# Who issues the roll: the two partition-shift transfers of q, k and v move from SyncE's queue to ScalarE's

## The reference

```python
def _to_quaternion(x):                       # x: (B, S, 16 heads, 8)
    p1 = jnp.diff(x, axis=1, prepend=x[:, :1])   # difference along the sequence
    p2 = jnp.roll(x, 1, axis=2)                  # heads shifted by one
    p3 = jnp.cos(x)
    return jnp.stack([x, p1, p2, p3], axis=-1)

qkv = (x @ aw + ab).reshape(B, S, H, 3 * HD)
q, k, v = jnp.split(qkv, 3, axis=-1)
qk = _hamilton(_to_quaternion(q), _to_quaternion(k))
qkv_p = _hamilton(qk, _to_quaternion(v))
... # spectral filter over positions and heads, projection, residual, norm, feed-forward
x = L0_attn_x
xn = _layernorm(x)
x = x + _L0_attn_ref(xn, ...) + _L0_ffn_ref(xn, ...)
xn = _layernorm(x)
x = x + _L1_attn_ref(xn, ...) + _L1_ffn_ref(xn, ...)
```

## Time and profile before

| | |
|---|---|
| median of three runs | 1510.28 us (1504.66 to 1510.45) |
| the profiled execution's own time | 1511.32 us |
| its span | 1509.5 us |
| granted TensorE clock, mean | 0.977 |
| PE busy | 1401.4 us (93%) |
| DVE busy | 1253.8 us (83%) |
| ACT busy | 1044.0 us (69%) |
| POOL busy | 356.2 us (24%) |

### The profile page before, as it was taken

The page is one execution under the profiler, slowest core; times in us unless marked ns, Lnnn a source line. Parts: engine busy times, 40 slices in busy tenths (PEclk is TensorE's granted clock), DMA queues, the critical chain, the costliest instruction groups (busy, mean ns, idle before and its releaser), DMA issues.

```text
span 1509.5 us, 20944 instructions
## 1 busy us (share of the span) xinstructions
PE 1401.4 (93%) x6198; PEld 994.5 (66%) x6198; DVE 1253.8 (83%) x1575; ACT 1044.0 (69%) x2411; POOL 356.2 (24%) x251
## 2 busy tenths in 40 slices
PE   6999998999999999899999899999889999999858
PEld 4677766666566666566665666656677777777636
DVE  3344467877999989899959897999999999999985
ACT  6455757676787768766878767777857787776652
POOL 0001203110211412011131411131543344344410
PEclk9999999999999999999999899999999999999979
DMA  7663445345545554543364335355555566555235
GB/s 269 253 261 139 157 145 192 110 121 168 163 135 162 179 160 129 177 125 112 100 227 120 95 107 165 123 154 172 161 186 169 157 183 195 166 160 176 69 94 172
DMA packets 111244, 238.03 MB, mean 158 GB/s; under 512 B 13207, under 2 KB 52844, under 8 KB 109644
## 3 DMA queue, kind: packets, MB, share of 16 engines
q1 hardware_dynamic: 106588, 227.31, 47.8%
q0 software_dynamic: 4544, 9.38, 1.8%
HBM read 185.59 MB, written 43.86 MB: 152 GB/s over the span
## 4 chain that ended last, share of the span: by engine, by line
PE 41%; issue 22%; DVE 19%; ACT 9%; POOL 8%; DMA 2%; SPq 0%; ACTq 0%; DVEq 0%; POOLq 0%
PE bank L1353 8%; PE bank L1341 6%; PE bank L1343 6%; PE bank L1342 6%; POOL RSTD L1016 4%; PE bank L1530 3%; POOL ytok L1031 3%; DVE AM L1075 3%; DVE SH L1207 2%; ACT ROWS L856 2%; DVE TA L1071 2%; PE bank L1448 2%; DVE AM L1079 2%; DVE TA L1082 1%; ACT ROWS L869 1%
## 5 line engine op out<-in xcount | busy, mean ns | idle before, releaser
L1016 POOL TENSOR_TENSOR RSTD<-SS,power_half 128x4 f32<-128x4 f32 x96 | 157.0, 1635 | 825.5 <-ACT ROWS L856 825.3
L1353 PE MATMUL bank<-SH,WD 128*128 128x512 f32 x512 | 262.8, 595 | 0.2 <-DVE X L1223 0.2
L1341 PE MATMUL bank<-NH,GU 128*128 128x512 f32 x512 | 244.7, 478 | 0.9 <-DVE SH L1207 0.9
L1207 DVE TENSOR_TENSOR SH<-SH,bank 128x512 f32<-128x512 f32 x256 | 172.1, 681 | 75.0 <-ACT SH L844 44.6
L1071 DVE TENSOR_TENSOR TA<-QKV 128x2048 f32<-128x2048 f32 x96 | 219.5, 2287 | 1.2
L1343 PE MATMUL bank<-NL,GU 128*128 128x512 f32 x512 | 202.5, 395 | 0.0
L1342 PE MATMUL bank<-NH,GU 128*128 128x512 f32 x512 | 201.7, 394 | 0.0
L844 ACT ACTIVATE SH<-bank 128x512 f32<-128x512 f32 x256 | 153.0, 605 | 59.2 <-PE bank L1343 57.0
L1075 DVE TENSOR_TENSOR AM<-AM,TA 128x1024 f32<-128x1024 f32 x128 | 153.2, 1218 | 0.7
L1565 PE MATMUL bank<-XT,GU 128*128 128x256 f32 x624 | 148.0, 382 | 0.4 <-DVE SH L1325 0.4
L869 ACT ACTIVATE ROWS<-bank,RSTD 128x128 f32<-128x128 f32 x384 | 109.9, 373 | 53.5 <-POOL RSTD L1016 48.1
(11 more groups left out here) (233 smaller groups left out, 2855.8 us busy)
## 6 DMA issues: line engine op xcount, KB each, us to landing
GU<-halves SPq DMA_DIRECT2D x112, 512.0 KB, 4.2
QKV<-QKV SPq DMA_DIRECT2D x32, 720.0 KB
GU<-in_w_gu SPq DMA_DIRECT2D x39, 512.0 KB, 3.7
xg<-in_c_fill SPq DMA_DIRECT2D x8, 2080.0 KB
WD<-in_w_d SPq DMA_DIRECT2D x128, 128.0 KB, 2.2
FC<-ready_w SPq DMA_DIRECT2D x32, 512.0 KB, 5.2
WQ<-ready_w SPq DMA_DIRECT2D x32, 384.0 KB, 4.7
WD<-in_w_d SPq DMA_DIRECT2D x39, 256.0 KB, 3.8
```

The costliest lines, as they stand in the source:

```text
L1016: pool.tensor_tensor(RSTD[:], SS[:], (power_one if k[0] == "at" else power_half)[:], ALU.pow).then_inc(power_done, 1)
L1207: dve.tensor_tensor(SH[:, g % 4, :], SH[:, g % 4, :], banks[2 + g % 2][:], ALU.mult).then_inc(h_ready, 1)
L1341: pe.matmul(out, w_hi, x_hi, start=True, stop=False)
L1353: pe.matmul(banks[4][:], WD1[:, slot, :], SH[:, g % 4, :], start=first, stop=last).then_inc(down_done, 1)
```

## The change

The `roll` step stays in the planner's list, as a step of SP with the same place in every order, but SP no longer does anything there. The two transfers and their wait are written into ACT's `views` step with j = 2, behind the third view and its edge copies.

```diff
@@ block.sync @@
-            elif name == "roll":
-
-                h, m = half_of[k], HEAD
-                sp.wait_ge(view_read, upto("views", k + (2,)))
-                src, dst = own(QKV[:, h, :, 0, :]), own(QKV[:, h, :, 2, :])
-                sp.dma_start(dst[m:P], src[0:P - m]).then_inc(rolled[h], 16)
-                sp.dma_start(dst[0:m], src[P - m:P]).then_inc(rolled[h], 16)
@@ block.scalar, views, j == 2 @@
                         act.wait_ge(view_read, n + 1)
                         act.activation(EDGE[:, l, :, :], QKV[:, h, :, 0, TILE:TILE + 1], ACT.Copy).then_inc(edge_kept, 1)
                         act.activation(QKV[:, h, :, 0, 0:1], QKV[:, h, :, 0, 1:2], ACT.Copy).then_inc(edge_done, 1)
+                    act.wait_ge(view_read, n + 1)
+                    src, dst, m = own(QKV[:, h, :, 0, :]), own(QKV[:, h, :, 2, :]), HEAD
+                    act.dma_start(dst[m:P], src[0:P - m]).then_inc(rolled[h], 16)
+                    act.dma_start(dst[0:m], src[P - m:P]).then_inc(rolled[h], 16)
```

## The result

The changed kernel takes 1548.09 us (median of 4 runs, 1546.93 to 1549.0) against 1508.94 for the kernel before; the ratio is 1.0261 with a 95% interval of 1.0248 to 1.0275. That is 39 us slower, where I had forecast 14 and a range that ended at 1538. The direction was right, the size was not.

A forecast was written before the change was run, and what follows sets the result against it. No single engine bounds the whole span; PE is busiest to 1090 us, DVE nearly full after. Losses of 17.3 us less 3.0 gained at MP gave +14.3 on the 1510.3 median, about 1524 us (+0.9%), range 1507 to 1538.

The forecast's parts named there:

- What the roll costs where it is: SP's two issues take 1.66 us a roll, 53 in all; for 31 of 32 rolls the transfer is hidden.
- What the move adds on ACT: Behind the third view ACT's sequencer takes both issues: 1.66 us a roll, 1.45 in a sequence's first-tile passes.
- dearer: Rival: ACT's issues also queue while SP issues, some 1.6 us more on half or all rolls; 1533 to 1541 us, chance 0.13.
- the share of ACT's delay that passes on: How much of each roll's 1.66 us on ACT reaches waiting DVE, POOL and PE; losses summed to 17.3 us.
- the 12 late rolls: Twenty-first to last roll, where DVE idles 17 of 390 us: 0.7 us each passes on, 8.4 in all.
- the 15 rolls of the first stage off the chain: Between 200 and 1090 us, DVE's idle 105 us takes up most of a slip: 0.25 us each, 3.8 in all.
- the four on it: Sixth, ninth and sixteenth rolls at 1.45 us each, nineteenth at 0.8, where the chain runs through ACT: 5.1 us.
- The twenty-sixth roll: Late-stage example: DVE multiplies 0.14 us behind ACT's SiLU at 1241.59, so 1.45 us later means 1.3 us new DVE idle time.
- What the move gives back at `MP`: At the eleventh roll SP issues MP 3.3 us sooner, so PE's 3.0 us wait goes if the transfer still takes 13.4.
- The fourteenth roll: First Hamilton product waits 3.2 us for the landing anyway, so later cosines cost 0; passing SP's ring backlog would return 1.6.
- main forecast: Whole kernel: part of ACT's delay passes on, net +14.3 us, about 1524; own range 1515 to 1534, chance 0.52.
- the signs I named: ACT lists both issues; DVE's late SiLU waits over 10 us, idle about 25; SP's standing and PE's MP wait gone; more cosine waits.

The follow-up runs named there:

- the copy of 1990: Kernel before, roll still on SP; ACT also waits for the third view, then copies 1990 elements a partition to an unread scratch tile; ratio 1.0256.

## Why the prediction was wrong in size, point by point

- *What the roll costs where it is*: right. The kernel with the wait alone is unchanged, and the roll on SP was hidden.
- *What the move adds on ACT*: right. I took 1.66 us a roll; the issues last 0.92 + 0.72. With the gaps around them ACT was held up 1.69 us longer than before. I left open whether the issues would run beside ACT's computing: behind the third view they do not, behind the rounding they do. No issue stood in line for long: the longest of 32 took 1.50 us, all other large ones near 0.92. The *dearer* rival, and with it the Trainium skill's locked generator ("Perfetto Trace Analysis", the HWDGE part), would have added about 1.6 us to many rolls; nothing of that size shows on ACT. It shows on SP: of its nine issues that start less than 0.6 us behind the end of ACT's pair, eight take 1.86 to 2.49 us, as the one behind the roll did in SP's own queue before. So the price of the rival on ACT is near nothing, and the loss came to more than the rival's 1541 by another way.
- *The step that failed* is the share of ACT's delay that passes on, two terms of the sum. For the 12 late rolls I took 0.7 us each, 8.4 in all; measured alone they cost 16.9. For the 15 rolls of the first stage off the chain I took 0.25 each, 3.8 in all, and 5.1 for the four on it; those 20 rolls cost 22.5 net and about 28 before the step back of 5.9 at `MP` (below), 1.4 each. The ground I gave was that DVE is idle 12% of the first stage "so most of a slip is taken up". That idle time is no reserve: 64 of the 105 us are waits for ACT, and they move along with the delay. They grew to 92, and DVE's idle time in that stage by 24 us, on top of the 105. And I read the chain as if a roll off it were nearly free; the changed kernel's chain has 14% of ACT in place of 9%.
- *The shape* was not in the sum at all. I had one share per stage. The doses show that 0.61 us passes 0.23 of itself and 1.69 passes 0.73. My 0.25 us a roll would have been right for the large transfer alone, which cost 0.24.
- *The twenty-sixth roll*: the size was right, the instruction was not. DVE's timeline there, where before DVE went from one to the other without a pause:

```profile
1270.17 0.67 DVE L1322 TENSOR_TENSOR SH<-SH,bank 128x512 f32<-128x512 f32 x1
1272.13 0.69 DVE L1243 TENSOR_TENSOR XSL<-bank,XSH 128x512 fp32r<-128x512 f32 x1 [1.29 <-ACT XSH L896]
```

  1.29 us of new idle time against the 1.3 I gave, but in front of the low half `XSL`, which waits for ACT's `XSH`, and not in front of the multiplication. I had paired the wrong rows: by the order of the steps the multiplication at 1242.35 takes the SiLU of 1239.64, done 2.1 us earlier, and the SiLU at 1241.59 is multiplied at 1243.55. The consumer that was close was `XSL` at 1242.95, 0.25 us behind the end of `XSH`. So the kind of mechanism held, a consumer on DVE within a few tenths behind ACT; that the row I gave for it led to the same number was luck.
- *What the move gives back at `MP`*: less than I gave, and the wait went for another reason as well. PE's rows at that place, before and then after, with the window of before (its last three figures are granted clock, DMA share, GB/s):

```profile
634.17 6.60 PE L1530 MATMUL bank<-GE,MP 128*128 128x512 f32 x8 [3.03 <-DMA MP<-in_w_mproj]
...
634.00:641.00 7.00, 6.83 (x10) 3.06 (x11) 1.68 (x2) 1.20 (x5) 0.02 (x1) 0.57 0.32 129
```

```profile
646.00 3.70 PE L1527 MATMUL bank<-GE,MP 128*128 128x512 f32 x8
```

  The wait of 3.03 us was followed by eight products at a granted clock of 0.57 on average, most of the window at the lower level of 1.2 GHz, which took 6.60 us in place of 3.70. The shift of the changed kernel's trace is 14.8 us ahead of the wait, 11.8 at the first product and 8.9 at the end of the eighth (640.77 to 649.70), a step back of 5.9 in all. But the kernel with the copy of 1990, whose roll is still on SP, steps back by 4.5 at the same place, and the kernel with the wait alone by 3.2. Their rows, in that order:

```profile
646.29 3.70 PE L1537 MATMUL bank<-GE,MP 128*128 128x512 f32 x8 [1.41 <-DMA MP<-in_w_mproj]
...
633.07 3.70 PE L1531 MATMUL bank<-GE,MP 128*128 128x512 f32 x8 [2.67 <-DMA MP<-in_w_mproj]
```

  So ACT's delay alone, which makes PE later, took some 1.6 us off the wait in these executions, and the move of the roll at most the last 1.4. SP did issue `MP` 3.3 us sooner behind the view, as I had it. But the issue took 2.14 us in place of 0.43, and the transfer landed 15.4 us after its issue began in place of 13.4, at 645.95, 0.05 us before PE took it: my condition that it "still takes 13.4" failed. And the slow clock is not a fixed price of the wait: behind waits of 1.98, 2.78 and 3.05 us in three other kernels the eight products took 5.40 us, behind waits of 2.52 and 2.67 they took 3.70. The 6.60 us belong to the one profiled execution of the kernel before. The term of 3.0 was thus about twice too large for the move itself, which made the net forecast a little too fast.
- *The fourteenth roll*: unchanged, as the main forecast had it. The product waits 4.00 us in the changed kernel:

```profile
801.39 0.61 ACT L968 ACTIVATE QKV<-TURNS 128x512 f32<-128x512 f32 x1
...
805.60 2.29 DVE L1062 TENSOR_TENSOR AM<-QKV 128x2048 f32<-128x2048 f32 x1 [4.00 <-issue]
```

  The cosines end at 802.00 and the product starts 3.6 us later. The roll, issued at 792.25, is thus some 13 us under way, as against at most 11.4 before (issued behind the view, product at 791.21). From the view's end to the product it is 13.4 us here, and 11.4 to 13.6 in five profiled kernels with the roll in SP's queue. A ring of its own did not carry it past the fill that SP had issued 11.8 us earlier. The Trainium skill's account of the rings ("DMA: Bandwidth & Descriptors", "Queues, rings and completion order") may well be right; that the roll gains by it here, the trace does not bear out.
- Of the signs I named, the issues on ACT, DVE's waits for the SiLU (4.2 to 12.3 us, forecast over 10) and DVE's late idle time (27 us, forecast 25) came. The product's waits for the cosines did not grow: 1.8 us, five times, as before, and the wait at the fourteenth roll did not shrink.

## What to carry to other kernels

Idle time of an engine is not slack unless it would be idle for another reason: before counting it as cover for a delay, ask whether what ends it passes through the engine that is being delayed. To price extra time on an engine that feeds others at short range, put a dummy instruction of two or three lengths at that place; here the cost was about a quarter of the delay up to 0.9 us a pass and all of any addition beyond 1.4, so no one share can be carried from a short delay to a long one. A transfer that a computing engine issues right behind a wait for its own last result stops that engine for the whole issue; the same issue behind a wait that has long been met ran beside the computing, and its price was then only the later landing (15 us against 39). Here the queue of the engine that computes nothing was still the best place, even with 120 us of standing there.

## What the runs showed of the hardware that I had not expected

- An issue of the same transfer takes the same time on ACT as on SP, 0.92 and 0.72 us. Behind a wait for the view just made, it blocks ACT's computing: 1.81 us from the view to the SiLU in the timeline above, where only the edge copies, queued ahead of it, run beside it. Behind the rounding, with its wait long met, it does not: ACT's next instruction comes 0.12 us behind the rounding on average.
- SP's issue right behind the roll is long whatever it loads: of 17 that follow it within 0.12 us in the kernel before, 16 take 1.90 to 2.30 us and one takes 0.45. The same shows when the roll is ACT's: in the changed kernel `WP` and the fill, issued beside ACT's pair (628.80 to 630.48), take 0.32 and 0.72 us, and `MP`, 0.06 us behind that pair's end, takes 2.14, where before `WP` behind the roll took 1.90 and `MP` behind the fill 0.43:

```profile
629.40 0.32 SPq L735 DMA_DIRECT2D WP<-ready_w  x1
629.77 0.72 SPq L713 DMA_DIRECT2D xg<-in_c_fill  x1
630.54 2.14 SPq L739 DMA_DIRECT2D MP<-in_w_mproj  x1
```

- A wait of PE of 2 to 3 us was followed by eight products that took 3.70, 5.40 or 6.60 us, in different profiled executions; the length of the wait did not order them. The granted clock around them was 1.00 where they took 3.70, 0.72 in a window of 6 us around one that took 5.40, and 0.57 around the one of 6.60.
